# A channel-pair convolution with cyclic pairs: 36 pairs of a head instead of 48, rows of x permuted, six heads' products moved to GpSimd

## What is computed

```
q = layernorm(x)                               # over the 256 columns
16 heads of 8 channels each; k = v = ctx
kv[i,j]  = ctx[i] * ctx[j]                     # for all i, j of a head, by position
out[i,j] = causal_conv(kv[i,j], ssm_kernel[h]) + D[h] * kv[i,j]
y[j]     = sum over i of out[i,j] * q[i]
x        = x + tanh(g_xattn) * y
```

```
gates    = renormalised top 2 of softmax(z @ router_w + router_b)
combined = sum over e of gates[e] * gelu(z @ expert_w[e] + expert_b[e])
x        = x + tanh(g_ffn) * (combined @ out_w + out_b)
```

## Time and profile before

| what | value |
|---|---|
| median of 3 runs | 129.73 us (128.84 to 130.03) |
| span of the profiled execution | 128.5 us |
| PE busy | 112.0 us (87%) |
| DVE busy | 100.8 us (78%) |
| POOL busy | 66.8 us (52%) |
| ACT busy | 54.2 us (42%) |

### The profile page before, as it was taken

The page is one execution under the profiler, slowest core; times in us unless marked ns, Lnnn a source line. Parts: engine busy times, 40 slices in busy tenths (PEclk is TensorE's granted clock), DMA queues, the critical chain, the costliest instruction groups (busy, mean ns, idle before and its releaser), DMA issues.

```text
span 128.5 us, 1981 instructions
## 1 busy us (share of the span) xinstructions
PE 112.0 (87%) x622; PEld 97.9 (76%) x622; DVE 100.8 (78%) x281; ACT 54.2 (42%) x133; POOL 66.8 (52%) x103
## 2 busy tenths in 40 slices
PE   4939999997969996999910799999999999999981
PEld 4929999996958995968800688887588888888970
DVE  0278599999989999999999964758679867569661
ACT  3213148343133536556500378585454343423430
POOL 2069990959999999599998007992000000000000
PEclk9995999999999999999995559999999999999999
DMA  3869999540033020020000000000000011011111
GB/s 103 244 177 260 361 349 281 173 160 3 0 82 82 5 78 7 0 82 5 0 0 0 3 0 0 0 0 0 5 0 0 0 46 36 0 41 46 41 68 57
DMA packets 9916, 8.97 MB, mean 70 GB/s; under 512 B 1290, under 2 KB 9906, under 8 KB 9906
## 3 DMA queue, kind: packets, MB, share of 16 engines
q1 hardware_dynamic: 8530, 7.80, 20.0%
q10 hardware_dynamic: 1376, 1.05, 2.8%
HBM read 7.77 MB, written 1.07 MB: 69 GB/s over the span
## 4 chain that ended last, share of the span: by engine, by line
PE 44%; POOL 21%; DMA 14%; DVE 8%; SPq 6%; ACT 2%; issue 2%; DVEq 0%; POOLq 0%
PE ring L767 11%; PE ring L769 11%; PE ring L768 10%; DMA rwlast<-in_L_ffn_router_w 5%; POOL ctx_t L407 5%; POOL w_lo_t L413 5%; POOL kv_t L359 4%; POOL kv_t L362 3%; POOL ctx_t L406 3%; DMA kpad_dram<-mix_t 3%; DMA ctx_t<-in_L_ffn_expert_w 3%; SPq L320 2%; DMA dcol<-in_L_xattn_D 2%; SPq L315 2%; DVE gate L950 2%
## 5 line engine op out<-in xcount | busy, mean ns | idle before, releaser
L767 PE MATMUL ring<-w_hi_t,zT_hi_t 128*128 128x512 f32 (+1 forms) x66 | 27.7, 420 | 6.7 <-DVE mix_t L993 6.7
L993 DVE SCALAR_TENSOR_TENSOR mix_t<-ring,gates_t,mix_t 128x256 f32<-128x256 f32 x55 | 26.4, 483 | 7.8 <-ACT ring L556 6.4
L556 ACT ACTIVATE ring<-ring 128x512 f32<-128x512 f32 (+1 forms) x33 | 18.8, 569 | 19.1 <-PE ring L769 19.1
L769 PE MATMUL ring<-w_hi_t,zT_lo_t 128*128 128x512 f32 (+1 forms) x66 | 26.2, 397 | 0.0
L768 PE MATMUL ring<-w_lo_t,zT_hi_t 128*128 128x512 f32 (+1 forms) x66 | 26.1, 395 | 0.0
L767 PEld LDWEIGHTS ring<-w_hi_t,zT_hi_t 128*128 128x128 f32 x66 | 13.0, 196 | 9.0 <-DVE mix_t L993 6.9
L690 PE MATMUL ring<-kv_t,toep_t 128*128 128x192 f32 x64 | 16.3, 337 | 1.4 <-POOL kv_t L362 1.4
L359 POOL TENSOR_TENSOR kv_t<-ctxT_t 128x256 f32<-128x256 f32 x23 | 14.5, 632 | 5.1 <-ACT ctxT_t L482 5.1
L691 PE MATMUL ring<-kv_t,toep_t 128*128 128x192 f32 x64 | 15.7, 328 | 0.0
L692 PE MATMUL ring<-kv_t,toep_t 128*128 128x192 f32 x64 | 15.6, 326 | 0.0
L769 PEld LDWEIGHTS ring<-w_hi_t,zT_lo_t 128*128 128x128 f32 x66 | 12.8, 194 | 2.8
(11 more groups left out here) (114 smaller groups left out, 197.9 us busy)
## 6 DMA issues: line engine op xcount, KB each, us to landing
ctx_t<-in_L_ffn_expert_w SPq DMA_DIRECT2D x8, 256.0 KB, 3.0
toep_t<-kpad_dram SPq DMA_DIRECT2D x3, 512.0 KB, 6.2
wlast_t<-in_L_ffn_expert_w SPq DMA_DIRECT2D x1, 1024.0 KB, 9.8
out<-x_t SPq DMA_DIRECT2D x8, 128.0 KB, 1.7
ctx_t<-in_ctx ACTq DMA_DIRECT2D x2, 256.0 KB, 2.9
x_t<-in_x ACTq DMA_DIRECT2D x2, 256.0 KB, 4.3
ctx_t<-in_ctx SPq DMA_DIRECT2D x2, 256.0 KB, 4.3
x_t<-in_x SPq DMA_DIRECT2D x2, 256.0 KB, 7.3
```

The source lines that it names most:

```text
L556: act.activation(y, y, ACT.Gelu_apprx_tanh).then_inc(gelu_ready, 1)
L767: pe.matmul(y, hi, whi, start=(c == 0), stop=False)
L769: last = pe.matmul(y, lo, whi, start=False, stop=(c == C - 1))
L993: dve.scalar_tensor_tensor(out=acc, in0=ring[n % RING][:, L * e:L * (e + 1)], scalar=gate, in1=acc, op0=ALU.mult, op1=ALU.add).then_inc(mi ...
```

## The change

- A head's pairs are taken in cyclic order: channel i with channel (i + d) mod 8 for d = 0 to 3, all i (32 pairs), and for d = 4 only i = 0 to 3 (4 pairs). That is 36 pairs. The convolution works on 4 x 36 = 144 columns. To read channel (i + d) mod 8 without a wrap, `ctxT_t` and `qT_t` hold 11 floats for a head, the first three channels once more behind the eight; a step reads them as overlapping windows (`windows`). ACT (and DVE, for one tile of the queries) writes these in more and smaller evacuations.
- The products of a step are 256 and 32 elements instead of 256 and 128. The query products are four instructions, of 256, 192, 32 and 32 elements, instead of three of 256, 128 and 128; the number of terms stays 512.
- A term of channel (i + d) mod 8 must be able to run over into the next row of `zq_t`, so a channel's column there becomes 16 x its number in the head + the head. Adjacent terms are written 16 floats apart (or 144, for d = 4). To match, the rows of x are loaded and the result stored in this order (`by_channel`), one transfer for each batch, and the queries' evacuations reorder them.
- `BY_VECTOR` goes from nine steps to three; steps 8, 13, 18, 23, 28 and 30 move to POOL. `SLOTS` goes from 8 to 5.

```diff
-SLOTS = 8
+SLOTS = 5
-BY_VECTOR = (0, 8, 13, 15, 18, 23, 24, 28, 30)
+BY_VECTOR = (0, 15, 24)
...
-    NP = HD * HD - HB * HB
-    NPU = HB * HD
+    ND = HB * HD
+    NP = ND + HB
+    HX = HD + HB - 1
...
-        ctxT_t = sb("ctxT_t", [P, G * CB * P])
-        qT_t = sb("qT_t", [P, G * CB * P])
+        ctxT_t = sb("ctxT_t", [P, G * CB * H * HX])
+        qT_t = sb("qT_t", [P, G * CB * H * HX])
...
+        def by_channel(src, b):
+            return bass.AP(src.tensor, b * S * L, [[L, HD], [HD * L, H], [1, L]])
+        def load_x(eng, i):
+            for b in range(BL * i, BL * (i + 1)):
+                eng.dma_start(xv[:, b, :], by_channel(x, b)).then_inc(x_in[b], 16)
...
+        def windows(tensor, g, h):
+            width = G * CB * H * HX
+            return bass.AP(tensor, (g * CB * H + h) * HX, [[width, P], [H * HX, CB], [1, HB], [1, HD]])
+        def head_major(bank, c):
+            return bank[:, C * P * c:C * P * (c + 1)].rearrange("p (b i h) -> p b h i", b=BL, h=H)
...
-                sp.dma_start(out[b], xv[:, b, :]).then_inc(results_out, 16)
+                sp.dma_start(by_channel(out, b), xv[:, b, :]).then_inc(results_out, 16)
...
-            head = ctxTm[:, g, :, HD * h:HD * (h + 1)]
-            lower = head[:, :, 0:HB]
-            upper = head[:, :, HB:HD]
+            head = ctxTm[:, g, :, h, 0:HD]
             dst = kv[:, n % SLOTS]
-            eng.tensor_tensor(dst[:, :, 0:NPU].rearrange("p a (i j) -> p a i j", i=HB),
-                              lower.unsqueeze(3).to_broadcast([P, CB, HB, HD]),
-                              head.unsqueeze(2).to_broadcast([P, CB, HB, HD]), ALU.mult)
-            eng.tensor_tensor(dst[:, :, NPU:NP].rearrange("p a (i j) -> p a i j", i=HB),
-                              upper.unsqueeze(3).to_broadcast([P, CB, HB, HB]),
-                              upper.unsqueeze(2).to_broadcast([P, CB, HB, HB]), ALU.mult).then_inc(done, 1)
+            eng.tensor_tensor(dst[:, :, 0:ND].rearrange("p a (d i) -> p a d i", d=HB),
+                              head.unsqueeze(2).to_broadcast([P, CB, HB, HD]), windows(ctxT_t, g, h), ALU.mult)
+            eng.tensor_tensor(dst[:, :, ND:NP], head[:, :, 0:HB], head[:, :, HB:HD], ALU.mult).then_inc(done, 1)
...
+            def evacuate_context(i):
...
+                src = red[i % 2][:, :].rearrange("p (c m i) -> p c m i", c=C, i=HD)
+                own = ctxT[:, g, :, BL * k * H:BL * (k + 1) * H, :]
+                act.activation(own[:, :, :, 0:HD], src, ACT.Copy).then_inc(context_evacuated, 1)
+                act.activation(own[:, :, :, HD:HX], src[:, :, :, 0:HX - HD], ACT.Copy).then_inc(context_evacuated, 1)
+            def evacuate_queries(i):
...
+                for c in range(C):
+                    src = head_major((zbank, obank)[i % 2], c)
+                    own = qT[:, g, c, BL * k * H:BL * (k + 1) * H, :].rearrange("p (b h) i -> p b h i", h=H)
+                    act.activation(own[:, :, :, 0:HD], src, ACT.Copy).then_inc(act_queries_evacuated, 1)
+                    act.activation(own[:, :, :, HD:HX], src[:, :, :, 0:HX - HD],
+                                   ACT.Copy).then_inc(act_queries_evacuated, 1)
...
-                rows_lo = y[:, :, 0:NPU].rearrange("p a (i j) -> p a i j", i=HB)
-                rows_hi = y[:, :, NPU:NP].rearrange("p a (i j) -> p a i j", i=HB)
-                q = qTm[:, g, :, HD * h:HD * (h + 1)]
-                dst = zq[:, g, :, :, HD * h:HD * (h + 1)]
-                dve.tensor_tensor(dst[:, :, 0:HB, :], rows_lo, q[:, :, 0:HB].unsqueeze(3).to_broadcast([P, CB, HB, HD]),
-                                  ALU.mult)
-                q_hi = q[:, :, HB:HD].unsqueeze(3).to_broadcast([P, CB, HB, HB])
-                dve.tensor_tensor(dst[:, :, HB:HD, HB:HD], rows_hi, q_hi, ALU.mult)
-                dve.tensor_tensor(dst[:, :, HB:HD, 0:HB], rows_lo[:, :, :, HB:HD].rearrange("p a i j -> p a j i"), q_hi,
+                pairs = y[:, :, 0:ND].rearrange("p a (d i) -> p a d i", d=HB)
+                far = y[:, :, ND:NP]
+                q = qTm[:, g, :, h, 0:HD]
+                def terms(first, outer, inner, count):
+                    at = g * CB * HD * P + h
+                    return bass.AP(zq_t, at + first, [[G * CB * HD * P, P], [HD * P, CB], *outer, [inner, count]])
+                dve.tensor_tensor(terms(HB * P, [[P, HB]], H, HD), pairs, windows(qT_t, g, h), ALU.mult)
+                dve.tensor_tensor(terms(H, [[P + H, HB - 1]], H, HD), pairs[:, :, 1:HB, :],
+                                  q.unsqueeze(2).to_broadcast([P, CB, HB - 1, HD]), ALU.mult)
+                dve.tensor_tensor(terms(0, [], P + H, HB), far, q[:, :, HB:HD], ALU.mult)
+                dve.tensor_tensor(terms((HB - 1) * P + HB * H, [], H, HB), far, q[:, :, 0:HB],
                                   ALU.mult).then_inc(read_out, 1)
```

60 lines of the change are left out of this document (31 added, 29 removed).

## The result

The changed kernel takes **134.66 us** (median of 4 runs, 132.44 to 135.43), the kernel before 129.69 us beside it. The ratio is 1.027 (95% interval 1.019 to 1.035): slower by 2 to 3.5%. I had forecast 141. The direction is right and the size is not: +5 us instead of +11. The medians count every execution, the ratios leave out those that came out long, so a ratio can lie beside that of two medians.

The account below looks back on a forecast made before the run. DVE first, POOL close behind, were taken to bound the convolution stretch. Query products +18.9, channel products -7.0, query copies +0.4 and idle time -1.1 gave +11.2 us: span 139.7, time 141 us, range 129.5 to 148.

Parts of the forecast that it names:

- TensorE's fewer columns: Convolution stretch: 144 columns for 192 save TensorE 7.7 us over 32 heads, counted as 0 because DVE and POOL hide it.
- The channel products: DVE in the convolution stretch: only two of its products stay there, at 0.7 us each, which saves 7.0 us.
- DVE's idle time goes: Convolution stretch: DVE's 1.1 us of idle time go when DVE alone sets the pace, -1.1 us.
- POOL: POOL's channel products after 28.16 us: 14 heads at 0.77 to 0.89 us, net +0.9 to +2.6 us, hidden behind DVE, so 0.
- rival 4: Convolution stretch: TensorE's granted clock falls to the lower level, 1.2 GHz; at most +4.5 us, 145.5 us; chance 0.05.
- the store: DVE's query products: scattered stores at twice the packed rate, 2.08 ns an element, 1.33 us a head for 0.74, +18.9 us.
- The bounds: DVE's query products: 0.80 us a head at the packed rate as low end, 1.47 at 2.36 ns an element as high end.
- the loads: Start: four more x loads, 0.5 us each on ACT's queue, 0.65 on SP's; bias landing 0 to 1.3 us later, hidden.
- What follows I move as a block: Everything behind the convolution stretch: unchanged in length, only shifted, since its gates wait for DVE after its last query product.
- Rival 1: Convolution stretch: the scattered store costs what a packed one does and POOL binds; net -0.3 to +1.4, 130.2 us; chance 0.18.
- Rival 2: POOL's products after 28.16 us: a head costs nearly its first instruction's 0.57 us alone; -3.1 us, 126.6 us; chance 0.11.

Follow-up runs that it names:

- a_nohalf: The changed kernel without its seven halving sums, TensorE adding all eight terms: 128.41 us, ratio 0.988 to the kernel before.
- b_nohalf: The kernel before without its seven halving sums, TensorE adding all eight terms: 123.42 us, ratio 0.950 to the kernel before.
- a_plain8_nohalf: The changed kernel with contiguous rows in its eight transfers of x and of the output, and without halving sums: 123.65 us, ratio 0.954.
- a_again: The changed kernel run once more, unaltered: 134.50 us, ratio 1.033 to the kernel before.

## Why the prediction was right and wrong

**Right.** *TensorE's fewer columns are worth nothing here*: its busy time falls by 4.4 us and the stretch stays. *The channel products*: the two left take 29.10 to 30.05 and 44.64 to 45.47 us, 1.8 in all, so 6.6 us are saved (7.0 forecast). *DVE's idle time goes*: 0.07 us is left. *POOL* at 0.78 us a head, the low end of 0.77 to 0.89, and its last product ends 1.7 us later after the first bias than before (25.96 for 24.25 us), inside +0.9 to +2.6. *The clock* stays at 1.00 in the stretch; rival 4 is out.

**The step that failed: the store.** The term of the query products, "twice the packed rate, 2.08 ns", 1.33 us a head, +18.9 us, is the one that made the forecast. It measures 0.95 us, 32 x 0.21 = +6.7 us. Two errors add. A scattered store costs 0.43 for 0.33 us at 256 elements, 1.3 times, not twice. And I charged the two 32-element products 0.13 us each, where they take 0.09. The bounds held the value, and the choice of the middle was not made from a row. With 0.95 in my own sum the stretch would have come out at +6.7 - 6.6 + 0.4 - 1.1 = -0.6 us. It came out at +0.3, with DVE's sums inside it 0.7 us longer (5.02 for 4.33).

**The step that I waved through: the loads.** "Two on ACT's queue at 0.5 us, ... before its use", "Rows stay 1 KB", hidden. The transfers take 0.77 us (ACT) and 0.96 us (SP) to issue, and the late landings move the first query product by 2.8 us in the profiled execution. I looked at one user of that queue, the tanh, and asked only whether it came before its use; it came at 11.21 us, and the query scales with it. The start has no cover: DVE is the bound from its first query product on, so whatever delays that one delays all. This is the loss of the kernel: +2.65 us when the x loads alone are put into the kernel before, and 4.0 to 4.8 us back when all permuted rows are taken out of the changed one, with or without halving sums. 0.9 us of the difference is the output: from the gates on, a_nohalf and b_nohalf reach the issue of the last output transfer after the same time (55.12 and 55.08 us), and from there it is 2.99 and 2.11 us to the end. The prediction has no term for it. The rest, 0.5 to 1.2 us, is open; a_nohalf also has a stretch 1.0 us longer than a_plain8_nohalf.

**"What follows I move as a block"** was not right either: 15.2 us became 14.4 or 17.9. The end looks unmoved, 57.9 for 58.1 us, because two things cancel: the last output transfer takes 0.9 us more, and the work up to it 1.1 us less. TensorE pauses for 3.36 us before the gates where it paused for 6.70, and its granted clock in the 6 us behind them is 0.72, a mix of both levels, instead of 0.50, the lower one.

In sum, of the profiled +2.1 us, start +2.80, stretch +0.34, tail -0.80, end -0.2. The medians differ by 5.0; the other 2.9 us are not in this profile. That of a_again, a longer execution, has the start at 19.50 us and a tail of 17.93. The sign of my forecast came from the store, and the sign of the result from the rows: the right side by luck. Rival 1 had the stretch right, at -0.3 to +1.4, though not its reason, since DVE and not POOL was full; it gave the loads 0 to 1.3 us, and missed most of the start. Rival 2 had the stretch at -3.1. The range held the time only because it was wide.

## What to carry to other kernels

Cost a pattern of a transfer as a change of its own, by its issue time and by everything queued behind it, when it lies ahead of the first instruction of the engine that sets the pace. That holds for the output too, at the other end of the program. Compare how many landing signals a transfer sends in either pattern: here 8 and 16. Between two far bounds, an experiment on the disputed instruction is worth more than a middle value; where there is none, say that the two ends are two cases. Before trimming the busiest stretch, look at the gap behind it: taking four halving sums out of the tail gave more than anything that was done to the stretch.

## What was not expected of the hardware

- A DVE store of 256 elements with a step of 2 floats costs no more than a packed one, one of 4, 8, 16 or 64 takes 1.3 to 1.4 times the packed instruction, one of 24 1.6 times; one SBUF input at a step of 16 costs more (0.49 us for 0.33) than a store at that step, and a PSUM input nothing.
- A transfer of 128 KB takes 0.48 us on average to issue on ACT's queue with rows in order, 0.77 with rows taken 8 apart, and small transfers behind it land later by more than that. It signals its landing 8 times instead of 16, and alone, at the end of the program, takes 3.0 us instead of 2.1 from its issue to the end.
- Two sums of 1024 elements with both inputs in SBUF took DVE 2.9, 6.1 or 13.1 us, by what POOL did beside them. In the lockout POOL keeps its undisturbed pace for over 11 us and DVE's first sum ends only when POOL has paused; when both advance, they end in turns, and POOL's instruction takes 1.78 us for 0.73.
